# Gated cross-attention with a mixture of experts: turns of the additions by expert, and a second result bank

## What is computed

```python
x = x + tanh(g_xattn) * attention(layernorm(x), ctx, w_q, w_kv, w_out, b_out)
n = layernorm(x)
probs = softmax(n @ Wr.T)
vals, idx = top_k(probs, 2)
gate = sum(one_hot(idx) * vals / vals.sum())          # (tokens, 8)
y = einsum(silu(einsum(n, W1)), W2)                   # per expert, 256 -> 1024 -> 256
x = x + tanh(g_ffn) * einsum(gate, y)
```

## Time and profile before

| | |
|---|---|
| median of 3 runs | 539.62 us (538.2 to 540.16) |
| profiled execution, span | 541.8 us |
| TensorE busy | 491.6 us (91%) |
| VectorE, ScalarE, GpSimd busy | 360.8, 372.0, 362.2 us |
| additions into `out` | 39, 64.5 us busy, 98.7 us idle before them |
| mean granted clock of TensorE | 0.974 of full |

### The profile page before, as it was taken

How to read it: one execution, slowest core, us unless ns; L and a number is a source line. 1 busy time by engine, 2 the same in 40 slices (tenths; PEclk the granted TensorE clock), 3 DMA queues, 4 the chain that set the end, 5 groups by cost and what they waited for, 6 DMA issues and landing times. The chain is left out here.

```text
span 541.8 us, 17418 instructions
## 1 busy us (share of the span) xinstructions
PE 491.6 (91%) x6630; PEld 435.8 (80%) x6630; DVE 360.8 (67%) x860; ACT 372.0 (69%) x577; POOL 362.2 (67%) x377
## 2 busy tenths in 40 slices
PE   2889699999999999998877898999999999999993
PEld 2867569887888978787666786888999999999992
DVE  5799899898889989888993455563434444444431
ACT  1888989998989989888846356555555564656550
POOL 5469688898989899898888376443443545444433
PEclk9999999999999999999878799999999999999998
DMA  7954225072542507144256326886787878778722
GB/s 290 395 176 152 103 79 181 29 252 64 175 142 90 200 30 255 43 166 131 88 195 211 133 90 238 238 253 196 218 261 216 266 221 252 229 240 238 206 31 29
DMA packets 35059, 94.84 MB, mean 175 GB/s; under 512 B 4508, under 2 KB 24476, under 8 KB 27646
## 3 DMA queue, kind: packets, MB, share of 16 engines
q1 hardware_dynamic: 25812, 82.79, 43.6%
q0 software_dynamic: 8592, 10.81, 10.4%
q10 hardware_dynamic: 576, 0.14, 0.1%
HBM read 74.45 MB, written 19.28 MB: 173 GB/s over the span
## 5 line engine op out<-in xcount | busy, mean ns | idle before, releaser
L710 POOL DMA_INDIRECT out<-yt,row_of x39 | 64.5, 1654 | 98.7 <-DMA out<-yt,row_of 77.4
L1505 DVE SCALAR_TENSOR_TENSOR hT<-hf,h_scale,hT 128x512 f16<-128x512 f32 x78 | 58.3, 750 | 94.3 <-ACT hT L996 80.2
L1669 PE MATMUL st_bank<-xsT,w_tile 128*128 128x128 f16 x1872 | 114.7, 221 | 2.6 <-ACT pT L864 1.1
L1669 PEld LDWEIGHTS st_bank<-xsT,w_tile 128*128 128x128 f16 x1872 | 110.4, 99 | 4.5 <-issue 2.9
L1669 PE MATMUL o_bank<-w2s,hT 128*128 x936 | 109.8, 273 | 3.2 <-issue 1.6
L1669 PEld LDWEIGHTS o_bank<-w2s,hT 128*128 128x128 f16 x936 | 89.4, 98 | 15.5 <-issue 5.6
L990 ACT ACTIVATE hf<-st_bank,z_scale 128x512 f32<-128x512 f32 x78 | 53.1, 681 | 48.1 <-PE st_bank L1669 39.8
L607 POOL TENSOR_TENSOR pT<-pT 120x512 f16<-120x512 f32 x64 | 77.6, 1225 | 11.0 <-ACT pT L864 10.8
L863 ACT ACTIVATE pT<-st_bank,exp_bias,logit_scale 120x512 f32<-120x512 f32 x64 | 50.2, 784 | 24.2 <-PE st_bank L1886 15.4
L996 ACT ACTIVATE hT<-hf,h_scale 128x512 f16<-128x512 f32 x78 | 56.3, 722 | 10.1 <-PE o_bank L1669 3.9
L652 POOL TENSOR_SCALAR stage<-stage,upw 128x512 f32<-128x512 f32 x32 | 56.3, 1759 | 4.1 <-ACT w_hi L963 4.0
(11 more groups left out here) (216 smaller groups left out, 937.8 us busy)
## 6 DMA issues: line engine op xcount, KB each, us to landing
w_tile<-w_split SPq DMA_DIRECT2D x39, 1024.0 KB
stage<-in_w SPq DMA_DIRECT2D x16, 1024.0 KB, 5.2
w_split<-w_hi SPq DMA_DIRECT2D x8, 512.0 KB
w_split<-stage SPq DMA_DIRECT2D x8, 512.0 KB
out<-x SPq DMA_DIRECT2D x17, 128.0 KB
xin<-in_x SPq DMA_DIRECT2D x8, 256.0 KB, 2.7
w2s<-in_wkv SPq DMA_DIRECT2D x2, 1024.0 KB, 11.9
xres<-in_x SPq DMA_DIRECT2D x16, 128.0 KB
```

What stands on the lines that cost most here:

```text
L710: pool.indirect_dma_start(out=out[0:rows], out_offset=bass.IndirectOffsetOnAxis(row_of[:, t:t + 1], 0), in_=yt[t % XG][:], in_offset=None, ...
L1505: nc.vector.scalar_tensor_tensor(out=hT[par][:, 1, 4 * a:4 * a + 4, :], in0=hf[par][:, 512 * a:512 * a + 512].rearrange("p (c n) -> p c n" ...
L1669: ins = pe.matmul(out, lhs[i](a), rhs[i](c), start=(i == 0 and a + c == 0), stop=(i == n - 1 and a == 1))
```

## The change

1. The additions are counted by two semaphores, one for even and one for odd tiles. `add(t)` waits for all additions before it where the expert of t isn't that of t - 1. Where it is the same, t - 1 is left out of the wait, since two tiles of one expert have no token in common. How far to wait is a number in the new table `add_wait`, which GpSimd loads into a register before the wait. Behind the wait stands a product of 128x1 elements whose result nobody reads (`turn_over`). The wait for the tile's own gate is now the last one. Tiles 1 and 2 wait by constants, as before.
2. VectorE makes the table (`add_turns`), four small instructions each for the first 13 tiles and for the other 26. Tiles without tokens count as experts of their own there. `expert_f` is no longer cut down to 7; that happens in the conversion to `expert_of`, and one instruction goes.
3. Odd tiles from 11 on have their product in `j_bank[0]`, one of the three banks of the attention, all others in `o_bank`. The product of tile t from 11 on waits for the gate of t - 2 in place of t - 1.

```diff
+        add_wait = sb("add_wait", [P, TILES], I32)
+        prior = sb("prior", [P, TILES + 1], F32)
+        turn_over = sb("turn_over", [P, TILES], F32)
...
-        s_bank, z_bank, y_bank = max_bank, st_bank, o_bank
+        s_bank, z_bank = max_bank, st_bank
+
+        def y_place(t):
+            return (j_bank[0] if t > LISTED and t % 2 else o_bank)[:, 0:D]
...
-        y_added = sem("y_added")
+        y_added = [sem(f"y_added{i}") for i in range(2)]
+        turns_done = sem("turns_done")
...
-            sp.wait_ge(y_added, 16 * TILES)
+            for i in range(2):
+                sp.wait_ge(y_added[i], 16 * ((TILES + 1 - i) // 2))
...
+                pool.iota(prior[:].rearrange("p (k i) -> p k i", i=2), [[16, (TILES + 1) // 2], [0, 2]], base=0,
+                          channel_multiplier=0, allow_small_or_imprecise_dtypes=True).then_inc(const_done, 1)
...
             def add(t):
                 rows = EARLY_B * N if t < EARLY else T + P
-                pool.wait_ge(y_done, t + 1)
                 if t in (0, EARLY):
                     for i in range(NT):
                         pool.wait_ge(x2_out[i], 16 * ((B if t else EARLY_B) + i))
-                if t:
-                    pool.wait_ge(y_added, 16 * t)
+                most = 16 * ((t + 1) // 2)
+                if t in (1, 2):
+                    pool.wait_ge(y_added[1 - t % 2], most)
+                elif t:
+                    if t in (3, EARLY):
+                        pool.wait_ge(turns_done, 1 + (t == EARLY))
+                    turn = pool.value_load(add_wait[0:1, t:t + 1], min_val=most - 16, max_val=most)
+                    pool.wait_ge(y_added[1 - t % 2], turn)
+                    pool.tensor_tensor(turn_over[:, t:t + 1], row_id[:], row_id[:], ALU.mult)
+                if t >= 2:
+                    pool.wait_ge(y_added[t % 2], 16 * (t // 2))
+                pool.wait_ge(y_done, t + 1)
                 pool.indirect_dma_start(out=out[0:rows], out_offset=bass.IndirectOffsetOnAxis(row_of[:, t:t + 1], 0),
-                                        in_=yt[t % XG][:], in_offset=None, compute_op=ALU.add).then_inc(y_added, 16)
+                                        in_=yt[t % XG][:], in_offset=None, compute_op=ALU.add).then_inc(y_added[t % 2], 16)
...
-                chain.link(nc.vector.tensor_scalar(expert_f[:, c], expert_f[:, c], float(E - 1), None, ALU.min))
-                nc.vector.tensor_copy(expert_of[:, c], expert_f[:, c]).then_inc(experts_done, 1)
+                nc.vector.tensor_scalar(expert_of[:, c], expert_f[:, c], float(E - 1), None, ALU.min).then_inc(experts_done, 1)
+
+            def add_turns(b, late):
+
+                if b != B - 1:
+                    return
+                c = part(late)
+                n, lo = c.stop - c.start, max(c.start, 1)
+                own = by_expert[:, 0:n, 0]
+                dve.wait_ge(const_done, CONSTS)
+                chain.link(nc.vector.scalar_tensor_tensor(out=own, in0=expert_f[:, c], scalar=float(E) - 0.5, in1=tile_id[:, c],
+                                                          op0=ALU.is_gt, op1=ALU.mult))
+                chain.link(nc.vector.tensor_tensor(expert_f[:, c], expert_f[:, c], own, ALU.add))
+                own = by_expert[:, 0:c.stop - lo, 0]
+                chain.link(nc.vector.tensor_tensor(own, expert_f[:, lo:c.stop], expert_f[:, lo - 1:c.stop - 1], ALU.is_equal))
+                nc.vector.scalar_tensor_tensor(out=add_wait[:, lo:c.stop], in0=own, scalar=-16.0, in1=prior[:, lo + 1:c.stop + 1],
+                                               op0=ALU.mult, op1=ALU.add).then_inc(turns_done, 1)
...
             def expert_scales(late):
+                dve.wait_ge(experts_done, 1 + late)
...
             def y_gated(t, buf):
                 dve.wait_ge(y_full, t + 1)
-                if not (isinstance(t, int) and t < XG):
-                    dve.wait_ge(y_added, t * 16 - 16 * (XG - 1))
-                nc.vector.tensor_scalar(yt[buf][:], y_bank[:, 0:D], gate_y[:, bass.ds(t, 1)], None,
+                if t >= XG:
+                    dve.wait_ge(y_added[t % 2], 16 * ((t - XG) // 2 + 1))
+                nc.vector.tensor_scalar(yt[buf][:], y_place(t), gate_y[:, bass.ds(t, 1)], None,
                                         ALU.mult).then_inc(y_done, 1)
...
                 tile_gates(p - 23, 1)
+                add_turns(p - 24, 1)
                 tile_low(p - 25, 10)
...
                 tile_low(p - 1, 4)
+                add_turns(p - 1, 0)
...
             def down_product(e, t, par):
                 pe.wait_ge(h_low, t * 2 + 2)
-                if not (isinstance(t, int) and t == 0):
-                    pe.wait_ge(y_done, t)
-                ins = three(y_bank[:, 0:D], [lambda a, fc=fc: hT[par][:, a, fc, :] for fc in range(FC)],
+                if t == LISTED + 1:
+                    pe.wait_ge(job_free, JOBS.n_free)
+                if t:
+                    pe.wait_ge(y_done, t - 1 if t > LISTED else t)
+                ins = three(y_place(t), [lambda a, fc=fc: hT[par][:, a, fc, :] for fc in range(FC)],
```

5 lines of the change are left out of this document (3 added, 2 removed).

## The result

The changed kernel takes **529.99 us** in the median (528.65 to 532.07, 6 runs), the kernel before 538.72 us beside it (535.28 to 540.16, 6 runs). The ratio is 0.988 with a 95% interval of 0.9848 to 0.9912. The forecast of 539.3 us and its range from 537.6 are both missed: the change gains 8.7 us by the medians and 6.5 by the ratio, where 0.3 was expected.

What follows compares the result with a forecast made beforehand. TensorE's 5.52 us tiles were taken as the bound, with a short tail of additions. Last addition 537.20 became 536.20 + 0.73 = 536.93, so -0.27 us from the 539.62 median: 539.3 us, 8 in 10 within 537.6 to 541.9.

Steps and rivals of the forecast that it cites:

- So there is at most a tail to be shortened, and no rate: TensorE's tiles set the pace; only the last additions could gain, 2.4 us, or 3.1 without the last product's wait.
- TensorE never feels this: Late additions don't hold TensorE: four `yt` buffers stand between, and near the end it waits for a gate once, 0.77 us.
- In the middle of the stream the separate bank gives nothing either.: Second result bank for odd tiles: no gain in the stream, since no wait for a gate is there to be removed.
- 21 of the 38 steps: Additions said to lose their wait for the one before, by expert counts; not the last three, whose tiles are empty.
- The tail.: Additions 36 to 38 stay chained; the last starts at 536.20 + s instead of 537.20, a gain of 1.0 us less s.
- s = +0.73 on VectorE: Four small VectorE operations ahead of tile 10's `xsT` delay TensorE's stream by 0.73 us, bounds 0 and 2.0.
- The start 0.75 us behind a gate: On GpSimd, an addition starts 0.75 us after its gate ends, taken from a landing as also a semaphore wait; between 0.30 and 1.0.
- Queued behind an addition are only gathers, which are several tiles early.: On GpSimd's queue, work added ahead of or behind additions delays only gathers that have tiles to spare.
- No catching up: Rival, 13%: beside streaming weights two additions in flight land no sooner than one after the other; +1.6 us, 541.2.
- GpSimd's sequence becomes the bound: Rival, 6%: a register load over 1.62 us makes GpSimd's work per tile exceed 5.52 us; at 3 us, +16 us, 556.
- a stall in the tail: Rival, 6%: an unexplained GpSimd stall among the last three additions is paid in full, +2.0 us, 541.3.
- The last steps are looser than I read: Rival, 5%: the landing of 37 doesn't hold addition 38, which starts 2.4 to 3.1 us sooner; 536.5 to 537.2.

Runs made afterwards that it cites:

- g7_again: The kernel before, unchanged, profiled a second time: 538.61 us, ratio 1.0013.
- e2_sems: The kernel before with two more semaphores declared, unused: 539.70 us, ratio 1.0003.
- h2_early: The kernel before with every gather from tile 14 on issued one tile earlier on GpSimd: 536.92 us, ratio 0.9969.
- h3_swap: The kernel before with each addition waiting for the addition before it first and for its gate last: 535.34 us, ratio 0.9988.
- g5_left: The kernel before without the additions of tiles 5, 6, 7 and 8, all others still in one chain: 531.75 us, ratio 0.989.
- g3_listed: The changed kernel with additions 11 to 38 waiting for all before them, only those of tiles 3 to 10 loosened: 531.18 us, ratio 0.9886.
- e1_room: The kernel before with the three new tensors declared but unused, 472 bytes per partition: 537.77 us, ratio 0.994.
- g1_bank: The kernel before with the second result bank for odd tiles from 11 on, all additions in one chain: 537.13 us, ratio 0.996.
- g2_overlap: The changed kernel with all results in one bank again, only the additions loosened: 530.51 us, ratio 0.9861.
- g6_behind: The changed kernel with the four VectorE operations moved between the two halves of xsT of tile 10: 529.49 us, ratio 0.9847.
- g4_late: The changed kernel with additions 1 to 10 waiting for all before them, only those from tile 11 on loosened: 529.08 us, ratio 0.9851.
- h1_order: g6_behind with the addition's wait for its gate moved one place earlier, ahead of the wait for the addition two tiles back: 528.32 us, ratio 0.9843.

## Why the prediction was wrong

**What bounds the kernel: the step that failed.** "So there is at most a tail to be shortened, and no rate" was read from the earlier trace rows, and the reading was right for that execution. It wasn't for the kernel. In that execution TensorE was 9 to 12 us later than in the others, 4 us of it by pauses for which the profile names no cause, so its gates came late and hid all but 2 to 3 us of the additions' delay. In g7_again and e2_sems the additions are the bound for over 100 us, 10 us behind in the stream and 7.7 at the end. "TensorE never feels this" falls as well: in five such kernels it needs 0.8 to 2.2 us more between gates 12 and 33 than in the loosened ones (g7_again 116.65 us against 115.88), and it waits there for gathered rows. The text compared span and median, found 2.2 us between them, carried them over and asked nothing further. But a time is 2.1 to 2.3 us longer than its span, not shorter: the profiled execution was over 4 us longer than the median run. The span alone was more than any of the three timed runs had shown. And the 4 to 6 us of constant delay over 20 tiles stood in the text as an argument for one rival only. Here an addition chain that was late by a constant amount through the stream didn't make up for it (g7_again, h2_early, h3_swap), and what took additions away or loosened them ahead of the stream moved the end (g5_left, g3_listed).

**How the gain comes about.** The delay at tile 38 falls from 7.7 us (e2_sems, g7_again) to 2.5, which is 5.2. The gates themselves come earlier: in the five chained kernels with gathers in their old place and full weights (e1, e2, g7, g1, h3) gate 38 ends at 523.5 us in the median, in the eight loosened ones with two banks at 520.7. That is 2.8 us, and the two together are 8.0. Of the 2.8, the missing wait before the last product is 0.8 (g2_overlap, with one bank, still has 0.77 there; g1_bank, among the five, has not), and what TensorE loses in the stream, with waits for gathered rows of 0.3 in g7_again and up to 1.3 at once in g1_bank, is 1.1 in the median of the five. The rest is scatter between profiles or isn't accounted for; g6_behind differs from the others of its kind by 2 us. Had the prediction's own steps been put on the gates of g7_again, they would have given 521.57 + 0.75 + 3.89 + 1.03 + 0.73 = 527.97 against 532.82, a gain of 4.9 us: sign and mechanism right, and faster by 0.9%.

**"In the middle of the stream the separate bank gives nothing either."** Right: g1_bank, 0.996 with 1 in its interval. That a wait for the landing of 37 would swallow the earlier last product is right too: g2_overlap's last addition starts 1.65 us behind its gate, the changed kernel's 2.63. Of the "21 of the 38 steps", tile 2 is one that keeps its wait, so 20 are loosened; the forecast doesn't hang on it.

**The tail.** Right to a few tenths. 37 starts with its gate, at 0.77; 38 one flight and 0.72 later (4.59 in all, forecast 3.89 + 1.03).

**s = +0.73 on VectorE.** Right: TensorE's wait grew by 0.77, and g6_behind takes it away.

**The start 0.75 us behind a gate.** The value held, 0.77, but not the thought that any semaphore wait has it. It is 0.28 when the wait that blocks isn't the last one ahead of the transfer.

**GpSimd.** The load is 0.29 with 0.15 and 0.02 behind it, less than on SP, and hidden; the product is 0.19 and its distance to the addition 0.37 to 0.7 where nothing else is waited for. TensorE never waited for them.

```profile
L724 POOLq TENSOR_LOAD <-add_wait x36: 284/289/502, 331.9 to 519.0; - x36
```

The Trainium skill, DMA: Bandwidth & Descriptors, section Latency and other measured facts, gives about 600 ns as a floor for such a load. The 36 loads here, at 284 to 502 ns, lie under it.

**"Queued behind an addition are only gathers, which are several tiles early."** Wrong. Behind additions 10 us late they land just as TensorE comes to them, and now and then later: 0.29 us of wait at 421.50 in g7_again, none in h2_early.

**The rivals.** "No catching up" fell: a delay of 5.5 us is gone in five tiles (g4_late), and two additions in flight do overlap beside the weights. The Trainium skill, DMA: Bandwidth & Descriptors, section Issuing engines are not separate DMA queues, has all transfers share 16 engines. No run here measures what that costs the overlap, but the time of this rival didn't follow from it: what the overlap hides is the flight, 3.7 to 6.7 us for 128 KB in a stretch that moves 239 GB/s. "GpSimd's sequence becomes the bound" and "a stall in the tail" didn't come. "The last steps are looser than I read" named the nearest number (536.5) for a reason that didn't hold. No rival said that the chain was later than its profile showed, and this was the case.

## What to carry to other kernels

Before a bound is read from a profile, see whether its span fits the timed runs; if it is as long as the longest of them or longer, the engine that looks like the bound may be the one that was disturbed, and what stands a few us behind it may be the real one. A chain of dependent transfers that is late by a constant amount beside a full engine isn't covered: count how late it is, ask where the delay was built up, and loosen it anywhere upstream of the end. In front of a transfer on GpSimd, let the semaphore that comes last not be the last one waited for.

## What was unexpected in the hardware

- Of several waits ahead of an indirect DMA on GpSimd, the last is dearer when it is the one that blocks: 0.71 to 0.77 us from the release to the transfer, against 0.22 to 0.28 when another wait blocked and the last was met already (g5_left, h1_order, h3_swap against g7_again and the changed kernel).
- In a steady stream the flight of an accumulating DMA was longer when it started within 1.1 us behind the issue of a tile's weights (median 6.1 us against 4.2 from 1.4 us on; g7_again, e1_room, e2_sems), and a delay of 10 us stayed for 21 tiles, whether a link was made 0.47 us shorter, its gathers were moved, or, but for 2 us, half the weights' bytes were left out.
- One profiled execution had groups of TensorE's products torn apart by pauses of 0.3 to 0.5 us without a releaser, in four of the attention's eight batches, which made it 4 us late; it was 10 to 12 us late by tile 10. 18 other profiles, of kernels with the same products there, had none.
